# Block 1's ranks two up-layer pieces later, block 2's rows normalised in two parts, the third piece's low parts ahead of the long table, and another transfer order around unit 0

## What is computed

```python
# layer A: masked attention of h_target (2048 x 256) over x, 8 heads of 32, then a feed-forward part
q = (norm(h_target) @ Wq + bq).reshape(T, 8, 32) / sqrt(32)
k = (norm(x) @ Wk + bk).reshape(S, 8, 32);  v = ...
probs = softmax(where(adj != 0, q @ k.T, -1e30))          # adj is 2048 x 2048 int32, the same for all heads
ht = norm(ht + (probs @ v) @ Wo + bo)
x = x + ht + gelu(ht @ W1) @ W2
# layer B: every row goes to its 2 best of 8 experts, weighted by a softmax of the two gate values
gate = norm(x) @ gate_w.T
x = x + sum over the two experts of w_e * (gelu(norm(x) @ w1[e].T + b1[e]) @ w2[e].T + b2[e])
```

## Time and profile before

| | us |
|---|---|
| median of 3 runs (lowest, highest) | 1032.76 (1031.65, 1034.44) |
| the profiled execution | 1033.02 |
| its span in the trace | 1031.3 |
| PE busy in the span | 940.7 (91%) |
| ACT busy | 726.9 (70%) |
| DVE busy | 675.4 (65%) |
| POOL busy | 549.8 (53%) |

### The profile page before, as it was taken

How to read it: one execution, slowest core, us unless ns; L and a number is a source line. 1 busy time by engine, 2 the same in 40 slices (tenths; PEclk the granted TensorE clock), 3 DMA queues, 4 the chain that set the end, 5 groups by cost and what they waited for, 6 DMA issues and landing times.

```text
span 1031.3 us, 20809 instructions
## 1 busy us (share of the span) xinstructions
PE 940.7 (91%) x6750; PEld 570.8 (55%) x6750; DVE 675.4 (65%) x2002; ACT 726.9 (70%) x913; POOL 549.8 (53%) x485
## 2 busy tenths in 40 slices
PE   1788899999999999999999999989867899999993
PEld 1355444444444444444444445457556799898872
DVE  6759577887787978778787865656653644344331
ACT  3536789989999899998999994844414555555551
POOL 5647387575766667675666888201554422322311
PEclk9899899999999999999999999999986999999997
DMA  9587675754438553566267455681535222322323
GB/s 290 164 253 207 162 229 184 267 189 151 167 123 283 180 196 123 173 225 238 100 226 252 151 177 196 257 350 59 170 122 179 65 49 44 63 45 41 52 34 97
DMA packets 74298, 168.43 MB, mean 163 GB/s; under 512 B 13586, under 2 KB 42386, under 8 KB 68242
## 3 DMA queue, kind: packets, MB, share of 16 engines
q1 hardware_dynamic: 50354, 97.99, 29.1%
q0 software_dynamic: 19984, 67.93, 22.0%
q10 hardware_dynamic: 3856, 1.19, 0.5%
HBM read 120.84 MB, written 61.96 MB: 177 GB/s over the span
## 4 chain that ended last, share of the span: by engine, by line
PE 65%; DVE 10%; POOL 7%; DMA 6%; issue 5%; ACT 4%; SPq 2%; POOLq 0%; DVEq 0%; ACTq 0%
PE ps L1785 12%; PE ps L1948 10%; PE ps L1960 9%; PE ps L1822 9%; PE ps L1808 9%; PE ps L1810 9%; PE ps L1876 2%; DVE masked L1069 2%; POOL whl L776 2%; DMA split_weights<-whl 2%; PE ps L1864 1%; PE ps L1759 1%; DMA xs<-in_x 1%; DVE maskA L1031 1%; POOL whl L774 1%
## 5 line engine op out<-in xcount | busy, mean ns | idle before, releaser
L1069 DVE CUSTOM_DVE_ANT_0 masked<-ps,maskA 128x512 f32<-128x512 f32 x512 | 346.3, 688 | 106.5 <-PE ps L1785 104.3
L1584 ACT ACTIVATE masked<-masked,negmax 128x2048 f32<-128x2048 f32 x128 | 256.7, 2005 | 33.4 <-DVE negmax L1075 30.7
L1785 PE MATMUL ps<-ks,qs 96*128 96x512 f32 x512 | 257.3, 536 | 13.1 <-DVE piecemax L1069 9.1
L1687 ACT ACTIVATE weights<-ps 128x1024 f32<-128x1024 f32 x256 | 248.6, 1010 | 25.7 <-PE ps L1810 25.3
L1808 PE MATMUL ps<-qs,ks 98*128 98x512 f32 x512 | 226.9, 502 | 3.4 <-DMA qs<-shift_lo 3.1
L1810 PE MATMUL ps<-maskB,identb 128*128 128x512 bf16 x512 | 202.1, 395 | 0.0
L1785 PEld LDWEIGHTS ps<-ks,qs 96*128 96x128 f32 x512 | 99.0, 193 | 97.3 <-DVE piecemax L1069 77.8
L955 POOL DMA_INDIRECT sum_rows<-y,ids x39 | 60.2, 1543 | 154.8 <-DVE y L1300 131.0
L1822 PE MATMUL ps<-weights,v_all 128*32 128x256 f32 x2048 | 137.7, 387 | 0.0
L795 POOL TENSOR_SCALAR maskB<-adjB 128x1024 bf16<-128x1024 int32 x32 | 116.5, 3642 | 36.8 <-DMA adjB<-in_adjT 33.4
L1282 DVE TENSOR_TENSOR gT<-ffn_w,gT 128x2048 f16<-128x2048 f32 (+1 forms) x23 | 45.2, 1967 | 120.1 <-ACT gT L1641 120.1
(11 more groups left out here) (231 smaller groups left out, 1155.5 us busy)
## 6 DMA issues: line engine op xcount, KB each, us to landing
expert_rows<-pad_rows POOLq DMA_DIRECT2D x73, 272.0 KB, 5.8
split_weights<-whl POOLq DMA_DIRECT2D x36, 512.0 KB, 3.4
adjA<-in_adj SPq DMA_DIRECT2D x16, 1024.0 KB, 7.2
adjB<-in_adjT SPq DMA_DIRECT2D x32, 512.0 KB, 6.0
wall<-split_weights SPq DMA_DIRECT2D x16, 1024.0 KB, 16.0
wch<-in_w1T POOLq DMA_DIRECT2D x14, 512.0 KB, 5.6
wch<-in_w2T POOLq DMA_DIRECT2D x14, 512.0 KB, 6.0
xr<-expert_rows SPq DMA_DIRECT2D x16, 272.0 KB, 2.8
```

What stands on the lines that cost most here:

```text
L1069: dve.tensor_tensor_reduce(masked[:, a % 2, k * 512:(k + 1) * 512], ps[:, u % 2, :], maskA[:, a, k * 512:(k + 1) * 512], 1.0, NO_EDGE, ALU ...
L1584: act.activation(masked[:, a % 2, :], masked[:, a % 2, :], ACT.Exp, bias=negmax[:, h % 2, a:a + 1], accum_out=rowsum[:, h % 4, a:a + 1]).t ...
L1687: act.activation(weights[:, j % 4, :, :], ps[:, 2 + 2 * (j % 2):4 + 2 * (j % 2), :], ACT.Exp).then_inc(weights_ready, 1)
L1785: pe.matmul(ps[:, u % 2, :], qs[0:KR, h % 4, a * P:(a + 1) * P], ks[0:KR, h, k * 512:(k + 1) * 512], start=True, stop=True)\
```

## The change

Six edits, no instruction of work added or taken away, but one activation loop called in two parts:

- SP, prologue: `stack_query(0)` and its wait move ahead of the first two `next_adjB`.
- SP, unit 0: the loads `load_adjB(1, 0)` and `load_adjB(1, 1)` move from ahead of `store_shift(1)` to behind `load_inv(0)`.
- DVE: `send(1)` moves from behind low part 4 to behind low part 5 of block 3.
- DVE: `low_rows(2)` moves from behind `final_table` to ahead of `low_hidden(0)` and `final_table`.
- ACT: `normalise_x(2)`, which stood whole behind piece 6, is done in two halves, behind pieces 4 and 5.
- PE: `ranks(1)` moves from behind piece 4 to behind piece 6.

```diff
@@ SP, prologue
                 store_h(0)
                 store_h(1)
+                sp.wait_ge(kq_split, DC * NG + 1)
+                stack_query(0)
                 for h in range(2):
                     next_adjB(h)
-                sp.wait_ge(kq_split, DC * NG + 1)
-                stack_query(0)
                 stack_keys(1, back_cols)
@@ SP, loop
                     if n == 0:
                         for h_ in range(4, H):
                             stack_keys(h_, slice(0, T), (0, 2))
-                        sp.wait_ge(maskB_next, H - 1)
-                        load_adjB(1, 0)
                     elif n < 3:
                         store_queries(n + 1)
 
-                    if n + 1 + H < N:
+                    if n and n + 1 + H < N:
                         sp.wait_ge(maskB_next, n + H)
                         load_adjB(*divmod(n + 1 + H, H))
...
                     load_inv(n, b, h)
+                    if n == 0:
+                        for h_ in range(2):
+                            sp.wait_ge(maskB_next, H - 1 + h_)
+                            load_adjB(1, h_)
@@ DVE
-                    elif f == 4:
+                    elif f == 5:
                         send(1)
...
                 send(3)
+                low_rows(2)
                 low_hidden(0)
                 final_table()
                 dve.wait_ge(c_in, 32)
                 for j in range(SLOTS):
-                    if j + 2 < SLOTS:
+                    if 0 < j < SLOTS - 2:
                         low_rows(j + 2)
@@ ACT
-                def normalise_x(b):
+                def normalise_x(b, tiles=range(TPB)):
...
                     hidden_high(3, f)
-                    if f == 6:
-                        normalise_x(2)
+                    if f in (4, 5):
+                        normalise_x(2, range(2 * f - 8, 2 * f - 6))
@@ PE
                     hidden(3, f)
-                    if f == 4:
+                    if f == 6:
                         ranks(1)
```

More of the change, by code:

```diff
@@ L1595, in normalise_h @@
                     normalise(0, b, hb[:, b, :, :], hb[:, b, :, :], h2_normed, tiles)
-                def normalise_x(b):
+                def normalise_x(b, tiles=range(TPB)):
                     if b == 3:
                         act.wait_ge(scattered[1], 16 * TOPK * TPB)
-                    normalise(1, b, xb[:, b % 2, :, :], rows_of[b], xn_ready)
+                    normalise(1, b, xb[:, b % 2, :, :], rows_of[b], xn_ready, tiles)
                 def high_turned(b):
```

## The result

The changed kernel takes 1023.74 us (median of 5 runs, 1022.48 to 1026.36), the kernel before in the same comparison 1031.65 us (5 runs, 1026.98 to 1034.44). The ratio over all runs is 0.9933 (the two medians alone would give 0.9923), with a 95% interval of 0.9911 to 0.9955: 6.9 us faster, give or take 2.3. The forecast was 1021.8 with a range of 1018 to 1028. The profiled execution of the changed kernel took 1023.74 us and has a span of 1022.0 us, against 1031.3 before. In this document all runs count but one slow one of q1_unit0_mask_first, which took 3175 us where its eleven others took 1024 to 1035.

The account below looks back on a forecast made before the run. PE, busy 91% of the span, was taken as the bound, so only four gaps could shrink: 1.0 + 5.7 + 3.1 + 1.4 = 11.2 us off 1033.0 gives 1021.8 us, range 1018 to 1028.

Parts of the forecast that it names:

- rival 1: Prologue: by ring order the gap ahead of the queries makes later transfers land 1 us later; 1023.8 us, chance 0.25.
- signs of being wrong: ACT waiting 2 us or more for `q_low<-qq`, PE waiting for `shift_lo`, `scatter(2)` not 3 us earlier, among others.
- Prologue, -1.0 forecast: Queries ahead of two tiles: PE 5 us ahead early, mostly lost at `store_queries(1)`; -1.0 us, range -3 to +1.
- The open question: Prologue: whether `store_queries(1)` lands 2 to 3 us earlier, or no earlier and perhaps 1 us later.
- Unit 0, -5.7 forecast: Rows ahead of two tiles: unit 1's 3.1 us stall and 2.6 us of slowness go; -5.7 us, range -3 to -6.3.
- The 2.6 us for the slow stretch behind the stall: Unit 0 term: 3.0 us of slow PE work behind unit 1's stall goes, of which 2.6 us were counted.
- Cover: 2 us or more: Unit 0's price on POOL: masks 2 to 4 us later, with 2 us or more to spare before `store_shift(2)` is due.
- only the key transfers lie ahead: Unit 0 step: the moved rows follow only the key transfers and land about 121.1, PE needing them at 121.24.
- Block 3's up layer, -3.1 forecast: Ranks, send, normalise moved: ranks come without a wait, down products start at 748.8; -3.1 us, range -1.5 to -4.
- Expert part, -1.4 forecast: Low rows ahead of the table: PE's 2.90 us wait for `low_rows(2)` goes; -1.4 us, range -0.5 to -2.
- The new waits: Expert part: second_half(0) starts 0.95 us later, and second_half(1) must also await `weigh(0)` until 811.9.
- Rival 3: PE's slow stretches return behind the 0.95 us wait or in the up layer; last two edits give nothing; 1026.3, chance 0.08.

Follow-up runs that it names:

- q1_unit0_mask_first: Kernel before with unit 0's two rows ahead of two adjacency tiles, plus POOL making block 1's second mask ahead of the weight split; ratio 0.9971.
- p2: Kernel before with unit 0's part alone, two rows ahead of two adjacency tiles; ratio 0.9989.
- p3: Kernel before with block 3's up-layer part alone (DVE `send(1)` with the ACT and PE edits); ratio 0.9971.
- p4: Kernel before with the expert part alone (DVE `low_rows(2)` moved); ratio 0.9975.
- r1: Changed kernel without the prologue part; ratio to the kernel before 0.9949.
- q2: Changed kernel with `store_queries(1)` ahead of `next_adjB(2)`, the keys and `next_adjB(3)` in SP's prologue; ratio to the kernel before 0.9892.
- r0: The changed kernel run again for a second trace; ratio to the kernel before 0.9940.
- q3: Changed kernel with DVE's scale and shift of block 2 put behind low parts 2 and 4 of block 1's up layer; ratio to before 0.9893.
- q4: Changed kernel with POOL's mask first, SP's query stores earlier and DVE's scale and shift split; 1019.53 us, ratio to the kernel before 0.9856.
- r3: q4 with DVE's `turned_shift` two score pieces earlier in every unit; ratio to the kernel before 0.9910.

## Why the prediction was right, and where not

The time and its range held, in part by luck. The forecast was a gain of 11.2 us and 6.9 were timed; the time lies only 1.9 us off because the kernel before took 1031.65 us in the comparison, not the 1033.0 from which the sum was taken, and because the medians lie further apart than the ratio says. The measured 1023.74 is in fact rival 1's figure (1023.8), and not for its reason. Three of the prediction's own signs of being wrong came as well: ACT waited 5.16 us for `q_low<-qq`, PE waited 0.53 us for `shift_lo` in unit 2, and `scatter(2)` began only 0.45 us earlier against unit 31. Of the four terms the up layer's and the expert part's were right for their own reasons, the prologue's had the right mechanism and about the right size, unit 0's was right in this pair of traces and too large in general, and what was missing from the sum was a loss at a place that it hadn't looked at.

**Prologue, -1.0 forecast.** Right in mechanism: 5 us ahead early, all of it lost at the query store. Measured -0.15 in the pair; the five later traces of the old order (p2, p3, p4, q1, r1) have 51.99 to 52.74 us, mean 52.4, and the four of the new one (51.38 to 51.92) a mean of 51.7: -0.7. The first profile's 51.53 was an early one; with it the mean is 52.3 and the gain 0.5. The open question, whether the store would land earlier, ended at "no earlier". Rival 1 described this ending, with 1 us of loss; that loss didn't come.

**Unit 0, -5.7 forecast.** -5.1 in the pair, but 509.65 us was the slowest of four traces of the old order. Their mean is 508.1; with the new order p2, q2, r0, r1, q3 and the changed kernel have 507.1, 507.2, 504.7, 504.3, 504.1 and 504.6, mean 505.3. So the edit is worth some 2.8 us, and two steps failed. The 2.6 us for the slow stretch behind the stall was taken as fixed; the traces have 3.0, 1.6, 1.6 and 0. And the price was looked for on the masks ("Cover: 2 us or more"): those held nothing. It lay on the two rows of the next unit, which now go out beside POOL's 1.5 MB; waits of 0.4 to 1.8 us. The step "only the key transfers lie ahead" looked at SP's queue alone and left out that another queue's transfers share the engines. The Trainium skill (DMA: Bandwidth & Descriptors, Queues, rings and completion order) says that each DMA engine takes turns between the queues for which it has work; the rows' 5.3 us behind POOL's store and 2.8 to 3.0 us in unit 0 of q2, q4 and r3, where POOL sent nothing just ahead, agree; they show that the two queues share something, not in what order they are served.

**Block 3's up layer, -3.1 forecast.** Unit 31 to back(3, 0) takes 128.2 us in the old order and 124.7 to 124.9 in the new one where no slow stretch falls into it: -3.4. POOL's `gap` work, which had stood idle 3.92 us, now follows `scatter(1)` at once and 0.6 us later against the down products (9.81 us behind them, 9.22 before). `scatter(2)` begins 14.47 us behind them, and 14.40 before: nobody waited, as said.

**Expert part, -1.4 forecast.** -1.3 in p4, -0.8 to -1.1 in the changed kernel, where the low rows and the table came 0.4 us later, behind PE's slow first matmuls of `first_half(0)`. The new waits were named right: 0.89 us against 0.95, and 0.64 ahead of second_half(1).

**Rival 3 half came.** A slow stretch came back elsewhere and took 2.85 us, but not behind the new waits: behind an old one of 3.02 us, which had cost nothing extra in the profile before. With these sizes the sum is 0.7 + 2.8 + 3.4 + 1.0 = 7.9, less 0 to 2.85: 5.1 to 7.9 us, and 6.9 and 6.2 were timed.

## What to carry to other kernels

The idle time ahead of a row is its sure price; the slow matmuls behind it are a chance, and one profile shows one throw of it: cut the trace at fixed points and compare several runs before a term is taken from it. Where a transfer is moved to land in time, look at every queue's transfers beside its new place, not only at its own queue, since two engines' work that drifts past each other can collide in any of the first rounds, here in unit 2 or 3. A stall that nothing touches is still worth removing: here two vector operations, placed three and five pieces later, gave 2.4 us by themselves, and in none of the three traces with them did the slow stretch follow that cost up to 2.9 more.

## What the runs showed of the hardware

The same 3.02 us of idle PE was followed by full clock in five traces, by 1.35 to 1.65 us of loss in four and by 2.9 in two. The start of a program up to one and the same instruction varied by 3.2 us. The second of two rows of 2 KB landed 2.8 to 5.8 us after its issue where PE waited for it: 2.8 to 3.0 us in unit 0, 3.9 to 5.4 with POOL's 1.5 MB begun 1.5 to 3.7 us ahead, and 4.7 to 5.3 behind two tiles of 512 KB on SP's own queue. A query store of 256 KB that was issued 2.1 us earlier, but behind a tile load, landed no earlier.
